# Twelve layers of a two-way selective scan: the gate by a SiLU activation, scratch tiles swapped, preparation re-laid, and the residual added in DRAM by a GpSimd transfer

## What is computed

```python
def _ssm(x, dbc_w, dtp_w, dtp_b, A_log, Dp):
    A = -jnp.exp(A_log)
    dbc = jnp.einsum('bld,ed->ble', x, dbc_w)
    delta, Bm, Cm = jnp.split(dbc, [DT_RANK, DT_RANK + D_STATE], axis=-1)
    delta = jax.nn.softplus(jnp.einsum('blr,dr->bld', delta, dtp_w) + dtp_b)
    dA = jnp.exp(delta[..., None] * A)
    dBu = delta[..., None] * Bm[:, :, None, :] * x[..., None]
    # h = dA_t * h + dBu_t over the sequence; y = sum over the 16 states of h * C_t
    return y + x * Dp

def _block(x, p):
    skip = x
    xn = (x - mu) / jnp.sqrt(var + LN_EPS) * ln_g + ln_b
    xp = jnp.einsum('bld,ed->ble', xn, pw) + pb
    z = jax.nn.silu(xp)
    xf = jax.nn.softplus(jnp.einsum('bld,ed->ble', xp, cfw) + cfb)
    x1 = _ssm(xf, ...)
    xb = jax.nn.softplus(jnp.einsum('bld,ed->ble', xp[:, ::-1, :], cbw) + cbb)
    x2 = _ssm(xb, ...)[:, ::-1, :]
    return x1 * z + x2 * z + skip
```

## Time and profile before

| | us |
|---|---|
| median of 3 runs | 21882.45 (21880.83 to 21883.69) |
| the profiled execution, its own time | 21919.67 |
| its span, first to last instruction | 21917.8 |
| busy POOL, DVE, PE, ACT | 20726.1, 20326.0, 18480.5, 11667.5 |
| DMA, mean over the span | 182 GB/s |

### The profile page before, as it was taken

How to read it: one execution, slowest core, us unless ns; L and a number is a source line. 1 busy time by engine, 2 the same in 40 slices (tenths; PEclk the granted TensorE clock), 3 DMA queues, 4 the chain that set the end, 5 groups by cost and what they waited for, 6 DMA issues and landing times.

```text
span 21917.8 us, 192168 instructions
## 1 busy us (share of the span) xinstructions
PE 18480.5 (84%) x45506; PEld 7633.0 (35%) x46368; DVE 20326.0 (93%) x11964; ACT 11667.5 (53%) x12349; POOL 20726.1 (95%) x8269
## 2 busy tenths in 40 slices
PE   7888888888888888888888888888888888888887
PEld 3333333333333333333333333333333333333333
DVE  7999999999999999999999999999999999999999
ACT  5555555555555555555555555555555555555554
POOL 8999999999999999999999999999999999999999
PEclk9999999999999999999999999999999999999999
DMA  4555555555555555555555555555555555555555
GB/s 151 185 183 178 188 183 180 182 181 184 182 184 183 176 187 182 181 183 183 181 181 184 180 183 184 180 181 180 186 180 181 186 181 181 183 183 182 184 184 179
DMA packets 1125763, 3978.56 MB, mean 182 GB/s; under 512 B 148992, under 2 KB 159744, under 8 KB 1124352
## 3 DMA queue, kind: packets, MB, share of 16 engines
q1 hardware_dynamic: 1073664, 3926.33, 52.5%
q10 hardware_dynamic: 50688, 36.88, 0.7%
HBM read 3836.89 MB, written 125.83 MB: 181 GB/s over the span
## 4 chain that ended last, share of the span: by engine, by line
issue 32%; PE 21%; POOL 19%; DVE 18%; DMA 6%; ACT 2%; DVEq 1%; POOLq 0%; ACTq 0%; SPq 0%
DVE ring L834 13%; POOL ring L364 12%; PE y L677 11%; PE bank L695 6%; DVE bv L818 5%; PE bv L667 3%; DMA c<-c_rows 3%; DMA pre<-out_dram 2%; POOL delta L404 2%; POOL u L412 2%; POOL parts L394 1%; POOL v L372 1%; PE y L688 1%; ACT dA L503 1%; DVE w L848 1%
## 5 line engine op out<-in xcount | busy, mean ns | idle before, releaser
L364 POOL TENSOR_TENSOR ring<-ring,c 128x1024 f32<-128x1024 f32 x6144 | 14310.1, 2357 | 407.9 <-DVE ring L834 366.9
L677 PE MATMUL y<-ring,ident 128*128 128x512 f32 x24576 | 11793.3, 606 | 460.0 <-DVE z L840 272.3
L834 DVE TENSOR_TENSOR_SCAN ring<-dA,bv 128x1024 f32<-128x1024 f32 x5376 | 12027.8, 2271 | 159.2 <-ACT dA L503 58.9
L818 DVE TENSOR_TENSOR bv<-u,bv 128x1024 f32<-128x1024 f32 x5376 | 6391.9, 1215 | 1288.7 <-PE bv L667 1051.8
L503 ACT ACTIVATE dA<-delta,a_step 128x1024 f32<-128x1024 f32 x5376 | 5971.8, 1143 | 1726.0 <-DVE ring L834 1573.1
L677 PEld LDWEIGHTS y<-ring,ident 128*128 128x128 f32 x24576 | 4763.0, 195 | 4804.5 <-issue 3593.2
L667 PE MATMUL bv<-parts,select 128*128 128x512 bf16 x9890 | 3130.8, 392 | 2521.7 <-DVE ring L834 2448.0
L503 ACT ACTIVATE bv<-delta,a_step 128x1024 f32<-128x1024 f32 x768 | 856.8, 1116 | 4004.2 <-DVE ring L834 4004.2
L667 PEld LDWEIGHTS bv<-parts,select 128*128 128x128 bf16 x10752 | 776.3, 100 | 6297.3 <-DVE ring L834 5287.5
L372 POOL TENSOR_TENSOR v<-u,v 128x1024 f32<-128x1024 f32 x768 | 1809.2, 2356 | 652.8 <-DMA v<-c_rows 652.6
L834 DVE TENSOR_TENSOR_SCAN ring<-bv,v 128x1024 f32<-128x1024 f32 x768 | 1738.9, 2264 | 0.0
(11 more groups left out here) (66 smaller groups left out, 11966.2 us busy)
## 6 DMA issues: line engine op xcount, KB each, us to landing
c<-c_rows SPq DMA_DIRECT2D x6144, 512.0 KB, 4.4
v<-c_rows SPq DMA_DIRECT2D x768, 512.0 KB, 5.8
out_dram<-z SPq DMA_DIRECT2D x96, 1024.0 KB, 7.8
pre<-out_dram SPq DMA_DIRECT2D x88, 1024.0 KB, 7.6
w<-out_dram SPq DMA_DIRECT2D x88, 1024.0 KB, 6.5
c_rows<-dbc ACTq DMA_DIRECT2D x192, 128.0 KB, 2.2
pre<-in_x_dram SPq DMA_DIRECT2D x8, 1024.0 KB, 7.9
w<-in_x_dram SPq DMA_DIRECT2D x8, 1024.0 KB, 6.4
```

The lines of the kernel that those rows point to most:

```text
L364: nc.gpsimd.tensor_tensor(ring[k % NR][:], ring[k % NR][:], c_sb[k % NC][:], ALU.mult).then_inc(p_ready, 1)
L677: mm = pe.matmul(y[:, half(h)], ident[:], ring[k % NR][:, half(h)], start=(k % HALF_TILES == 0), stop=(k % HALF_TILES == HALF_TILES - 1), ...
L818: nc.vector.tensor_tensor(bv[k % 2][:], u_of(d, s)[:, c, :], bv[k % 2][:], ALU.mult).then_inc(v_ready, 1)
L834: nc.vector.tensor_tensor_scan(h, a, b, 0.0, ALU.mult, ALU.add).then_inc(h_ready, 1)
```

## The change

The gate becomes one Silu activation in place at ACT's tile 40, between two loads of the activation tables. `out` is primed with x by eight copies DRAM to DRAM at the start, so that every iteration's z can be added to it by a transfer that POOL issues at tile 5; the reload of w, POOL's residual add and SP's store are gone. The scratch of the two directions is swapped, so `pre` is free after the first delta, and x is loaded for the iteration after the next at SP's tile 50. The shared tiles, the distances to them and the tiles of nearly every step of the preparation are new numbers. Waits follow the new users of the buffers.

```diff
-    SHARED = (7, 15, 23, 31, 39, 47, 55, 63)
-    B_AHEAD, V_AHEAD = 4, 7
+    SHARED = (9, 19, 23, 29, 35, 45, 55, 59)
+    B_AHEAD, V_AHEAD = 5, 6
...
-    LAG, HELD = 5, 3
+    LAG, HELD = 5, 2
...
-    MEAN_AT, CENTRE_AT, SQUARE_AT = (1, 7), (9, 11), (8, 11)
-    VAR_AT, RSTD_AT, NORM_AT = (9, 11), (10, 12), (9, 12)
-    PROJ_AT, XP_AT = (15, 17, 19, 19), (16, 16, 20, 20)
-    CONV_AT = ((21, 23, 25, 27), (29, 31, 33, 35))
-    CONV_OUT_AT = ((22, 22, 28, 29), (29, 30, 32, 34))
-    XS_LOG_AT, XS_AT = ((29, 32), (35, 35)), (34, 39)
-    DBC_AT, DBC_OUT_AT = ((37, 39), (44, 46)), ((37, 39), (50, 50))
-    DTP_AT, DTP_OUT_AT = ((41, 41, 42, 43), (49, 49, 51, 51)), ((40, 40, 42, 42), (51, 51, 52, 52))
-    HI_AT, REST_AT, MID_AT, PARTS_AT = (41, 51), (45, 54), (48, 54), (47, 56)
-    DELTA_LOG_AT, DELTA_AT, U_AT = ((43, 46), (53, 55)), (46, 56), (48, 57)
-    DIAG_AT, A_STEP_AT = 53, 40
-    GATE_AT, GATE_MUL_AT = (2, 3, 9), 5
-    STORE_AT = 16
-    W_AT = 54
-    SKIPS = ((9, 7), (39, 46))
+    MEAN_AT, CENTRE_AT, SQUARE_AT = (3, 4), (8, 10), (7, 10)
+    VAR_AT, RSTD_AT, NORM_AT = (9, 11), (11, 15), (9, 16)
+    PROJ_AT, XP_AT = (15, 15, 19, 19), (16, 16, 19, 19)
+    CONV_AT = ((22, 23, 25, 27), (29, 31, 33, 35))
+    CONV_OUT_AT = ((21, 23, 28, 29), (29, 30, 33, 34))
+    XS_LOG_AT, XS_AT = ((31, 32), (35, 35)), (35, 39)
+    DBC_AT, DBC_OUT_AT = ((37, 39), (47, 49)), ((37, 39), (47, 48))
+    DTP_AT, DTP_OUT_AT = ((41, 41, 41, 42), (49, 51, 51, 51)), ((40, 41, 42, 42), (50, 50, 52, 52))
+    HI_AT, REST_AT, MID_AT, PARTS_AT = (40, 49), (44, 53), (45, 57), (47, 55)
+    DELTA_LOG_AT, DELTA_AT, U_AT = ((43, 47), (55, 55)), (47, 55), (47, 57)
+    DIAG_AT, A_STEP_AT = 49, 53
+    GATE_AT = 37
+    LOADX_AT = 50
+    W_AT = 55
+    SKIPS = ((13, 9), (51, 55))
...
-        scratch = (tmp, pre)
+        scratch = (pre, tmp)
...
             def load_x(n, src, b):
-                sp.wait_ge(delta_ready, n * 2)
+                if not early(n, 1):
+                    sp.wait_ge(delta_ready, (n - 1) * 2 + 1)
                 sp.dma_start(pre[:], src[b]).then_inc(x_loaded, 16)
...
-            def load_w(it, src, s, b):
-                sp.wait_ge(skip_summed, it * (DIRS * DT) + DIRS * DT)
-                sp.dma_start(w[s][:], src[b]).then_inc(w_loaded, 16)
-            def store(it, s, b):
-                sp.wait_ge(out_ready, it + 1)
-                sp.dma_start(out_d[b], z[s][:]).then_inc(stored, 16)
...
-                if more:
-                    load_x(it + 1, next_src, (b + 1) % NB)
...
                     load_c(it, k, s)
-                    if k == STORE_AT and not early(it, 1):
-                        store(it - 1, 1 - s, (b - 1) % NB)
-                    if k == 50:
-                        load_w(it, src, s, b)
+                    if k == LOADX_AT and ahead:
+                        if b < NB - 2:
+                            if src is out_d:
+                                sp.wait_ge(stored, (it + 3 - NB) * 16)
+                            load_x(it + 2, src, b + 2)
+                        else:
+                            sp.wait_ge(stored, (it + 3 - NB) * 16)
+                            load_x(it + 2, out_d, b + 2 - NB)
             load_x(0, x_d, 0)
             for b in range(NB):
-                step(b, b, x_d, x_d if b < NB - 1 else out_d)
+                sp.dma_start(out_d[b], x_d[b]).then_inc(primed, 16)
+            load_x(1, x_d, 1)
...
+            pool.wait_ge(primed, 16 * NB)
...
-                if k == GATE_MUL_AT:
-                    pool.wait_ge(gate_sig, it + 1)
-                    nc.gpsimd.tensor_tensor(z[s][:], z[s][:], tmp[:], ALU.mult).then_inc(gate_ready, 1)
-            def finish(it, s):
-                pool.wait_ge(gated, it * DT + DT)
-                pool.wait_ge(w_loaded, it * 16 + 16)
-                nc.gpsimd.tensor_tensor(z[s][:], z[s][:], w[s][:], ALU.add).then_inc(out_ready, 1)
+            def finish(it, s, b):
+                one = out_d[b] if isinstance(b, int) else out_d[bass.ds(b, 1)].rearrange("o p c t -> p (o c) t")
+                pool.dma_start(one, z[s][:], accum_op=ALU.add).then_inc(stored, 16)
...
                 for k in range(k0, k1):
+                    if k == FIRST - 1 and not early(it, 1):
+                        pool.wait_ge(gated, (it - 1) * DT + DT)
                     product(it, k, s)
...
-                        finish(it - 1, 1 - s)
-                    gate(k, it, s)
+                        finish(it - 1, 1 - s, ended)
...
+            def tail(it, s, b):
+                pool.wait_ge(gated, it * DT + DT)
+                nc.gpsimd.memset(v_sb[:, 0:1], 0.0)
+                finish(it, s, b)
...
-            def gate(k, it, s):
-                if k == GATE_AT[0]:
-                    act.wait_ge(delta_ready, it * 2 + 2)
-                    act.wait_ge(conv_ready, (it + 1) * (2 * FILLS))
-                    nc.scalar.activation(tmp[:], z[s][:], ACT.Exp, scale=-1.0).then_inc(gate_exp, 1)
...
+                if k == GATE_AT:
+                    nc.scalar.preload_act_table_set(SILU_TABLES)
+                    act.wait_ge(conv_ready, n * (2 * FILLS) + 2 * FILLS)
+                    nc.scalar.activation(z[s][:], z[s][:], ACT.Silu).then_inc(gate_ready, 1)
+                    nc.scalar.preload_act_table_set(TABLES)
...
             def rstd(n, h):
-                act.wait_ge(gate_ready, n)
+                act.wait_ge(delta_ready, n * 2)
...
                 for k in range(k0, k1):
+                    weights(k - AHEAD - W_AT)
                     tile_exp(it, k, s)
-                    gate(k, it, s)
-                    weights(k - AHEAD - W_AT)
```

More of the change, by code:

```diff
@@ L14 @@
 TABLES = "natural_log_exp_and_others"
+SILU_TABLES = "silu_and_others"
 def conv_seq_kernel(nc, x, ln_g, ln_b, proj_w, proj_b, convf_w, convf_b, convb_w, convb_b,
@@ L192, in conv_seq_kernel @@
         skip_summed = sem("skip_summed")
-        w_loaded = sem("w_loaded")
+        primed = sem("primed")
         a_ready = sem("a_ready")
         gated = sem("gated")
-        out_ready = sem("out_ready")
         da_ready = sem("da_ready")
@@ L243, in no_weights, with turn @@
                 pass
-            def turn(it, s, more, next_weights=no_weights):
+            def turn(it, b, s, more, next_weights=no_weights):
                 slots(it, s, first, TILES, more > 0, next_weights)
                 if more:
-                    slots(it + 1, 1 - s, 0, first, more > 1, no_weights)
+                    slots(it + 1, 1 - s, 0, first, more > 1, no_weights, b)
                 else:
-                    tail(it, s)
+                    tail(it, s, b)
             load_raw(0)
@@ L262, in run_layers @@
                     it = layer * NB + pair * 2
-                    turn(it, 0, 2)
-                    turn(it + 1, 1, 2)
+                    turn(it, pair * 2, 0, 2)
+                    turn(it + 1, pair * 2 + 1, 1, 2)
                 it = layer * NB + (NB - 2)
-                turn(it, 0, 2, lambda part: weights(part, layer + 1, it + 2))
-                turn(it + 1, 1, 2)
+                turn(it, NB - 2, 0, 2, lambda part: weights(part, layer + 1, it + 2))
+                turn(it + 1, NB - 1, 1, 2)
             last = (LAYERS - 1) * NB
@@ L270, in run_layers @@
                 it = pair * 2 + last
-                turn(it, 0, 2)
-                turn(it + 1, 1, 2)
-            turn(last + NB - 2, 0, 1)
-            turn(last + NB - 1, 1, 0)
+                turn(it, pair * 2, 0, 2)
+                turn(it + 1, pair * 2 + 1, 1, 2)
+            turn(last + NB - 2, NB - 2, 0, 1)
+            turn(last + NB - 1, NB - 1, 1, 0)
         def nothing(*_):
@@ L321, in step @@
                     load_c(it, k, s)
-                    if k == STORE_AT and not early(it, 1):
-                        store(it - 1, 1 - s, (b - 1) % NB)
-                    if k == 50:
-                        load_w(it, src, s, b)
+                    if k == LOADX_AT and ahead:
[6 more added lines that the diff above has]
+                            load_x(it + 2, out_d, b + 2 - NB)
             load_x(0, x_d, 0)
             for b in range(NB):
-                step(b, b, x_d, x_d if b < NB - 1 else out_d)
+                sp.dma_start(out_d[b], x_d[b]).then_inc(primed, 16)
+            load_x(1, x_d, 1)
+            for b in range(NB):
+                step(b, b, x_d)
             with sp.Fori(1, LAYERS - 1) as layer:
                 for b in range(NB):
-                    step(layer * NB + b, b, out_d, out_d)
+                    step(layer * NB + b, b, out_d)
             last = (LAYERS - 1) * NB
             for b in range(NB):
-                step(last + b, b, out_d, out_d, b < NB - 1)
-            store(last + NB - 1, 1, NB - 1)
+                step(last + b, b, out_d, b < NB - 2)
             sp.wait_ge(stored, 16 * (last + NB))
@@ L549, in prepare @@
                                 act.wait_ge(proj_ready, n * FILLS + FILLS)
```

(11 more changed lines are left out.)

20 lines of the change are left out of this document (5 added, 15 removed).

## The result

The changed kernel takes 21361.07 us (median of 4 runs, 21350.82 to 21369.71), 0.9762 of the time before (95% interval 0.9745 to 0.9779), 2.4% faster; the forecast was 21400. The time agrees with the forecast. One of all the runs, of e6_lateu, took 26584 us at a granted clock of 0.689; the medians and ratios leave it out.

What follows compares the result with a forecast made beforehand. POOL with its v waits (222.7 us an iteration) bound the kernel, DVE close behind; afterwards ring B, 218.1. 96 times 5.2 gives 499 us, 484 net: 21919.7 to 21436, less 37 for the profiled run, 21400 us; range 21100 to 21700.

Steps and rivals of the forecast that it cites:

- the 484 of the sum: Whole kernel: 499 us gained over 96 iterations, less 10 for start-up and 5 for the last transfer.
- p: POOL's issue of the accumulating transfer at tile 5: 1.5 us taken, from 0.37 to 4.5, costing nothing on the path.
- HELD's lack of effect: PE's order: HELD does nothing, since with LAG at 5 one add is due in each tile either way.
- it waits 8 to 10 us at v 23: POOL, total 208.3 us an iteration, was to have its slack before the v product of shared tile 23.
- The other two signs: Forecast wrong if quiet iterations are not 217 to 220 us, or the GpSimd issue takes over 8 us.
- Rings A and B: Closed waits through v loads: A by scan 19 and v 23, 216.9 us; B by scan 55 and v 59, 218.1.
- C: Not predicted, found afterwards: POOL's product 38 to u, then DVE's tile 0 to scan 38; 217.3 us.
- the gaps of four: Shared tiles 19 to 23 and 55 to 59: POOL asks for v two tiles ahead of the scan freeing its buffer.
- The 5.2 us an iteration: Predicted gain per iteration: 3.8 us in a quiet one, 1.4 from loop ends and layer weights.
- its 5.4: Iteration with a layer's weights: 5.4 us of DVE's weight steps behind scan 55 fall into its wait for u.
- the 13.8 us: POOL's delta, u, three products and a v product before it needs c loads queued behind x at tile 50.
- rival 1: Rings don't bind; DVE with PE waits sets 212.3 us: 20840 us, 18%. With the skill's v transfer, about 21150 us.

Runs made afterwards that it cites:

- e6_lateu: Changed kernel with u of the second direction's tiles made at POOL's tile 60 instead of 47: 21502.51 us, ratio 0.9833.
- e1_reload: Changed kernel with the old residual: w reloaded on SP, POOL's add at tile 5, SP's store at tile 16: 21374.82 us, ratio 0.9786.
- e2_oldgate: Changed kernel with the old gate: exp, log and exp on ACT, POOL's product at tile 5; transfer kept: 21360.25 us, ratio 0.9780.
- e5_shared61: Changed kernel with the last shared tile at 61 in place of 59: 21368.13 us, ratio 0.9775.
- e7_shared61_lateu: Changed kernel with the last shared tile at 61 and the second direction's u at POOL's tile 60: 21247.48 us, ratio 0.9718.
- e3_both: Changed kernel's order with both old operations back (old gate with product; reload, add and store): 21371.24 us, ratio 0.9786.
- e4_newops_oldorder: Kernel before with only Silu, its table loads, priming copies and accumulating transfer; old tile numbers and scratch: 21774.7 us, ratio 0.9973.
- e11_latex: Changed kernel with x loaded at the start of SP's step for the next iteration, scratch still swapped: 21354.78 us, ratio 0.9747.

## Why the prediction was right, and where it was wrong

- *The time.* 21400 predicted, 21361 measured; a quiet iteration 218.1 against 217.8 in the trace. The gain of a layer of eight iterations was put at 42 us; by the gates it went from 1819 to 1770 or 1771, 48 us. The closeness of 21400 to 21361 is in part luck. From profile to profile 550 us went, not the 484 of the sum; but I took 37 us off for the distance of the profiled execution from the median, and in the changed kernel that distance is 9 us, so an error of 66 us shows as one of 39.
- *Right: POOL's work.* 206.8 us and p was the sum, 208.1 us is the busy time, with p at 0.98 us for the 1.5 taken (the products are a little slower, 14334.4 us for 14310.1). That p costs nothing on the path is shown by e1_reload, with 4.5 us in its place.
- *Right: the gate on ACT.* The load, the Silu and the second load follow each other without a gap, 4.52 us in the trace of a quiet iteration, and e2_oldgate is no faster:

```profile
9996.97 1.28 ACT L573 ACT_TABLE_LOAD   x1
9998.27 1.91 ACT L575 ACTIVATE z<-z 128x2048 f32<-128x2048 f32 x1
10000.20 1.28 ACT L576 ACT_TABLE_LOAD   x1
10001.49 2.19 ACT L492 ACTIVATE dA<-delta,a_step 128x1024 f32<-128x1024 f32 x2
```

  The Trainium skill (ScalarE: Activation LUTs, What ACT_TABLE_LOAD costs) has about 2.66 us for a switch with its drain. Here the load takes 1.28 us with no gap of more than 0.02 us around it, and the trace decides.
- *Right: PE's order.* 1.1 us at tile 25 measured 1.26, 1.3 us at tile 54 measured 1.60. The 0.7 us behind tile 9 did not appear; 0.68 us at tile 3 did, which I had not listed. HELD's lack of effect was argued from the code and not run.
- *Wrong: where POOL's slack is.* The step "it waits 8 to 10 us at v 23" failed. NORM_AT is 9 but RSTD_AT is 11, which is ACT's tile 14, so POOL waits for ACT before the norm: 7.9 us an iteration. I took the wait lists of the changed steps for v, x and the gate, and not for this pair. After it POOL waits 0.82 us before v 23. By the prediction's own sign (wrong if POOL's v waits are under 3 us an iteration) this part is refuted: they are 1.3 us (120.9 over 96). The other two signs hold: quiet iterations of 217.8 us, and 0.98 us for the GpSimd issue.
- *Wrong: which ring binds.* Rings A and B were said to set the time; e5_shared61 refutes B alone. The measured one is C, through POOL's unbroken 84.3 us up to u. That ring B's sum, with its 6.1 us for the load of v, hit the iteration to 0.3 us was luck: in the iteration shown above POOL doesn't wait for v 59 at all. The three sums lie near each other since every ring goes round the same DVE work with POOL's burst in it (216.9, 218.1 and 217.3 us), so the agreement confirmed none of them. That the gaps of four are a near second bound is shown by e6_lateu with e7_shared61_lateu.
- *Wrong: what the change's parts are worth.* I began with POOL's 9.1 us saved as the core. e3_both shows that the time saved on POOL is worth next to nothing in the new order, and e4_newops_oldorder 0.3% in the old one. The early load of x, which I counted among the repairs, is worth nothing that shows either (e11_latex): with the mean matmuls at tile 3 the late load does not hold PE up.
- *Wrong in size: loop ends and weights.* The 5.2 us an iteration were 3.8 for a quiet one and 1.4 for loop ends and weights. By the gates of eleven layers a quiet iteration gained 4.9 us. I counted four loop ends in eight iterations, worth 1.5 us each on top; three intervals of eight are longer, and they went from 228.9 us to 220.4, 4.7 more than the 3.8. The iteration with the weights was to gain 9.2 us, its 5.4 among them; it went from 242.1 to 238.5, 3.6. DVE does not wait for u in it, as I had said, but its own steps for the weights grew from 220.5 to 257.2 us over the kernel. The start came 20.5 us later (first gate at 257.55 us against 237.02) for the 10 taken, and not through POOL's wait for the copies. And the 13.8 us that POOL has before it needs the loads of c leave out the delta that the sentence names; with its 4.5 they are 18.3, and nothing in the sum goes by them. The figure that rival 1 takes from the Trainium skill (DMA: Bandwidth & Descriptors, Anatomy of one DMA) is given in that section for transfers that GpSimd issues, while v is loaded by SP. Its 21150 us rests on that figure alone.

## What to carry to other kernels

When two engines are both over 90% busy, work taken from one is not time gained: first follow the ring of waits that closes once in an iteration, and see on which engine the removed work stood in slack. An iteration's engine order in a software pipeline can be worth more than its operations: here the two distances (0.7%) and the places of the shared tiles (1.0%) each gained more than 750 us less of POOL work. A single relaxed bound can show nothing (e5_shared61), or a loss (e6_lateu); two near-equal ones must be relaxed together. And a sum that comes out does not show that its ring is the one that binds.
